# Runs of three chunks in place of four in a one-hot adjacency build

## The chip, the cores and the metric

The kernel runs on one core of one Trainium2 chip. The metric is the device time of one execution in microseconds (us), the median over several runs. Five engines work at once, each with its own instruction stream, and meet through semaphores: TensorE (PE; its weight loads are shown as PEld), VectorE (DVE), ScalarE (ACT), GpSimd (POOL) and SyncE (SP).

## The reference

The kernel computes two layers of a graph network over 3125 nodes with 256 features: a graph convolution, an attention and a feed-forward part in each. What matters here is the graph: 100,000 edges (src, dst), sorted by dst. Both graph convolutions need sums over the edges that end in a node.

```python
dst = jnp.minimum((3125 * jax.random.uniform(jax.random.fold_in(_gk, 3), (100000,)) ** 2.0).astype(jnp.int32), 49999)
_o = jnp.argsort(dst, stable=True)
src = src[_o]
dst = dst[_o]
...
def _gcn_conv(h, src, dst, norm, W, b, n):
    hw = h @ W
    msg = norm[:, None] * hw[src]
    return jax.ops.segment_sum(msg, dst, num_segments=n) + b
```

The square makes the targets uneven: low nodes have many edges, high nodes few.

## The kernel before, in words

The kernel first counts the edges between all pairs of nodes into a dense matrix, `adjacency`, in DRAM, and the graph convolutions later read it as an ordinary matrix. This case is about the stage that builds it.

The edges lie in 782 chunks of 128, one edge to a partition. The target nodes are split into 125 groups of 25 (25 tiles of TG = 5 groups). As the edges are sorted, a group's edges are a range of chunks that follow one another. A chunk at a border belongs to two groups. A preparation stage works out for each group its first chunk and its number of runs, where a run is RUN chunks and the last run of a group is filled up with chunks that aren't the group's (their keys match no column, so they add zeros). Each group has at least one run. It leaves (first, runs, runs before, runs up to) for each group in `ranges_row`, and the engines load these into registers (`ranges_of`, L469; the load is L472).

For a chunk two one-hot matrices are made: `hot_src` (128 edges x 125, the place of the source node, with a column of ones beside it for the degrees) and `hot_key` (128 x 625, target node and source block). TensorE multiplies the first by the second and adds into PSUM, in two pieces of 512 and 113 columns (L554). The engines share the work of the stage so:

- GpSimd copies a run's keys and sources into small buffers (L493, L496), up to AHEAD = 16 runs ahead.
- VectorE loops over all runs of all groups without knowing the groups. It makes the keys' one-hots of all chunks of a run (L519) and the sources' one-hots of all but the last (L516).
- ScalarE makes the source one-hot of a run's last chunk with two activations (square L577, relu L581). Group by group it also takes the finished sums out of PSUM (L590). It makes the sources of group g + 1 before it takes out group g.
- TensorE loops over the groups. For each it loads the range, waits for a free bank of sums, multiplies the block for the self-loops (L545), and then the chunks run by run.
- SyncE stores each group's sums to `adjacency` (L615).

`hot_src` and `hot_key` have RUN slots. The engines hold each other with `hot_ready` (a slot is filled) and `hot_used` (its chunk has been multiplied); chunk j of a run goes to slot j, so VectorE waits ahead of each slot until the chunk that was there one run before has been used:

```python
for j in range(RUN):
    dve.wait_ge(hot_used, n * RUN + (j + 1))
```

Behind the stage the degrees are summed from the stored matrix (L524 to L532). All stages are separated by barriers.

Of the kernel before, what the change touches and what calls it, by code (L numbers as in the profile page):

```python
# [25 lines left out]
HID = 512  # L26
E = 100000
CHUNKS = 782
RUN = 4
AHEAD = 16  # L30
CHUNKS_PAD = CHUNKS + RUN
GW = T * 25
# [43 lines left out]
def graph_kernel(nc, a, out):  # L76
    with ExitStack() as top:
# [132 lines left out]
        with ExitStack() as phase:  # L210
# [12 lines left out]
            with ExitStack() as prep, nc.Block() as block:  # L223
                def q(name, shape, dt=F32):
                    return prep.enter_context(nc.sbuf_tensor(name, shape, dt))
# [132 lines left out]
                def _(dve):  # L358
# [35 lines left out]
                    step(nc.vector.tensor_tensor(last[:], last[:], rng[:, 0:1], ALU.subtract))  # L394
                    step(nc.vector.tensor_scalar(last[:], last[:], 1.0 / RUN, (RUN - 1) / (2.0 * RUN), ALU.mult, ALU.add))
                    step(nc.vector.tensor_scalar(last[:], last[:], ROUND, ROUND, ALU.add, ALU.subtract))
# [36 lines left out]
            with ExitStack() as build, nc.Block() as block:  # L433
                def q(name, shape, dt=F32):
                    return build.enter_context(nc.sbuf_tensor(name, shape, dt))

                hot_src = q("hot_src", [128, RUN, P + 1], BF16)
                hot_key = q("hot_key", [128, RUN, GW], BF16)
                run_keys = q("run_keys", [128, AHEAD, RUN])
                run_srcs = q("run_srcs", [128, AHEAD, RUN])  # L440
                counts = q("counts", [128, TG, GW])
# [3224 lines left out]
```

How the kernel before makes its waits and increments, by code:

```python
            def __call__(self, ins, by_itself=False):  # L134
                self.n += 1
                ins.then_inc(self.sem, 1)
                if by_itself:
                    alone(self.eng, self.sem, self.base + self.n)
                else:
                    self.eng.wait_ge(self.sem, self.base + self.n)
# [7 lines left out]
            def settle(self):  # L148
                self.eng.wait_ge(self.sem, self.base + self.n)
# [14 lines left out]
        def alone(eng, signal, value):  # L164
            eng.wait_ge(signal, value)
            eng.sem_inc(waits_met, 1)
# [1 line left out]
        def load_all(eng, loads, landed):  # L170
            for dst, src in loads:
                eng.dma_start(dst, src).then_inc(landed, 16)
            eng.wait_ge(landed, 16 * len(loads))
# [18 lines left out]
            @block.gpsimd  # L192
            def _(pool):
                nc.gpsimd.memset(ident[:], 0.0).then_inc(const_made, 1)
                nc.gpsimd.memset(ones[:], 1.0).then_inc(const_made, 1)
                pool.wait_ge(const_made, 2)
                nc.gpsimd.affine_select(out=ident[:], in_=ident[:], compare_op=ALU.not_equal, fill=1.0, base=0,
                                        pattern=[[-1, 128]], channel_multiplier=1).then_inc(const_made, 1)
                pool.wait_ge(const_made, 3)
# [78 lines left out]
                @block.sync  # L278
# [1 line left out]
                    for dst, src in ((src_i, "src"), (dst_i, "dst")):  # L280
                        sp.dma_start(dst[:], a[src]).then_inc(landed, 16)
                    sp.wait_ge(cleared, 2)
                    for dst, src in ((edst_i, "edst"), (esrc_i, "esrc")):
```

## Time and profile before

| what | value |
|---|---|
| time of the kernel before, median of 3 runs | 4308.22 us (4301.39 to 4308.76) |
| span of the profiled execution | 4665.5 us |
| adjacency stage in it | 59.1 to 631.3 us, 572.2 us |
| VectorE busy in the stage | 483.1 us |
| TensorE busy in the stage | 476.0 us |
| ScalarE busy in the stage | 317.4 us |

The profiled execution is one execution with the recorder on, and no other time of its own is known than its span; it is 8.3% above the median of the timed runs. A row of the profile gives an engine, the line of the kernel, the operation with the tiles written and read, how often it ran, its busy time and the mean of one, and how long the engine stood idle just ahead of it and what ended that. Matmuls are pipelined and their ends are modelled; the starts of the weight loads (PEld) are the better marks of when TensorE went on.

### The profile page before, as it was taken

What the parts mean: (1) busy time and instruction counts of PE and PEld (TensorE: products, weight loads), DVE (VectorE), ACT (ScalarE), POOL (GpSimd) and SP (SyncE); (2) the same over time, 40 slices, a digit from 0 to 9 for tenths busy, and PEclk for the clock granted to TensorE, in tenths of its full rate; (3) what the DMA queues carried; (4) which work ended last, traced back from release to release, by engine and by line L of the source; (5) the groups of instructions that cost most, each with busy time, mean ns of one, the idle gap of its engine ahead of it and who ended that gap; (6) DMA issues with size and microseconds to landing.
All of it is one profiled execution on the core that took longest, in us unless ns stands there. A gap on an engine that the chain in (4) does not pass through costs nothing. (4 is left out here: it accounts for less than half of the span.)

```text
span 4665.5 us, 90783 instructions
## 1 busy us (share of the span) xinstructions
PE 3696.0 (79%) x23366; PEld 2634.7 (56%) x23367; DVE 2192.7 (47%) x5709; ACT 1348.5 (29%) x2983; POOL 739.5 (16%) x1224
## 2 busy tenths in 40 slices
PE   4888864899699989973464629859989899789998
PEld 2444433566388579651354416539879544457776
DVE  7888878888700221151263420270130677723333
ACT  2555532677700110320010203240000135233333
POOL 3222100000000000017423470200000466100000
PEclk9999975887799899986787859879999999989999
DMA  2111220323244024102010121224425100010000
GB/s 105 47 74 74 93 86 0 91 90 90 76 160 157 32 108 184 60 16 53 11 53 4 40 25 39 98 77 170 165 105 196 49 1 1 5 29 7 13 13 27
DMA packets 125733, 317.98 MB, mean 68 GB/s; under 512 B 43522, under 2 KB 76785, under 8 KB 111116
## 3 DMA queue, kind: packets, MB, share of 16 engines
q1 hardware_dynamic: 110404, 300.31, 18.5%
q0 software_dynamic: 11808, 9.68, 1.5%
q10 hardware_dynamic: 3404, 6.53, 0.4%
q8 instruction: 62, 1.02, 0.1%
q14 instruction: 55, 0.45, 0.0%
HBM read 244.21 MB, written 72.41 MB: 68 GB/s over the span
## 5 line engine op out<-in xcount | busy, mean ns | idle before, releaser
L554 PE MATMUL ps<-hot_key,hot_src 128*126 128x512 bf16 (+1 forms) x2208 | 416.9, 314 | 38.6 <-DVE hot_key L519 21.1
L519 DVE TENSOR_SCALAR hot_key<-col_iota,run_keys 128x625 bf16<-128x625 int16 x1104 | 393.7, 378 | 0.0
L2441 PE MATMUL ps<-xnT,ew 128*128 (+2 forms) x640 | 207.5, 479 | 206.7 <-issue 150.9
L1335 PE MATMUL ps<-gnn_u_thirds,near 125*128 125x256 bf16 x3000 | 334.7, 274 | 23.1 <-issue 23.1
L554 PEld LDWEIGHTS ps<-hot_key,hot_src 128*126 128x126 bf16 x2208 | 212.7, 136 | 234.2 <-DVE hot_key L519 171.7
L1335 PEld LDWEIGHTS ps<-gnn_u_thirds,near 125*128 125x128 bf16 x3000 | 329.7, 141 | 26.3 <-issue 24.7
L2441 PEld LDWEIGHTS ps<-xnT,ew 128*128 128x128 f32 x640 | 129.7, 210 | 279.2 <-issue 183.5
L2322 POOL DMA_INDIRECT rows_room<-node_table,src_idx x256 | 260.1, 1016 | 142.4 <-issue 142.4
L516 DVE TENSOR_SCALAR hot_src<-col_iota,run_srcs 128x125 bf16<-128x125 int16 x828 | 211.6, 256 | 97.4 <-PE ps L554 52.8
L863 PE MATMUL ps<-row_hot,slot_hot 128*128 128x512 f16 x1088 | 217.6, 351 | 3.1 <-DVE row_hot L1076 2.6
L2477 PE MATMUL ps<-table_thirds,rows_room 125*128 125x144 bf16 x1728 | 129.2, 232 | 113.9 <-issue 78.0
L2456 PE MATMUL ps<-ew,ehT 128*125 128x256 f32 x800 | 210.7, 409 | 0.0
L3620 DVE SCALAR_TENSOR_TENSOR xres<-ps,shares,xres 125x256 f32 x200 | 96.8, 484 | 239.5 <-PE ps L3585 218.6
L3574 PE MATMUL ps<-xnT,f 128*128 x640 | 185.5, 438 | 12.2 <-ACTq L3593 4.6
L1076 DVE TENSOR_SCALAR row_hot<-row_iota,row_of 128x670 f16<-128x670 int16 x544 | 189.4, 391 | 0.0
L2477 PEld LDWEIGHTS ps<-table_thirds,rows_room 125*128 125x128 bf16 x1728 | 114.2, 100 | 128.8 <-issue 128.4
L1335 PE MATMUL ps<-agg_u_thirds,near 125*128 125x257 bf16 x1500 | 175.4, 277 | 10.2 <-issue 9.7
L3574 PE MATMUL ps<-f_h1T,f 128*128 128x313 f32 (+1 forms) x640 | 180.1, 434 | 0.0
L3585 PE MATMUL ps<-fo,f_h2T 128*125 128x256 f32 x800 | 179.2, 379 | 0.0
L1335 PEld LDWEIGHTS ps<-agg_u_thirds,near 125*128 125x128 bf16 x1500 | 169.6, 141 | 16.6 <-issue 15.4
L1335 PE MATMUL ps<-gcn_u_thirds,near 125*128 125x256 bf16 x1500 | 166.6, 274 | 12.7 <-DVEq L1554 12.7
L3601 ACT ACTIVATE f_h1T<-ps,norm_shift,norm_scale 128x313 f32<-128x313 f32 (+1 forms) x160 | 98.0, 612 | 261.7 <-PE ps L3574 261.7
(570 smaller groups left out, 6651.9 us busy)
## 6 DMA issues: line engine op xcount, KB each, us to landing
near<-adjacency SPq DMA_DIRECT2D x80, 1562.5 KB, 6.6
adjacency<-counts SPq DMA_DIRECT2D x125, 312.5 KB, 2.2
own_in<-own_rows SPq DMA_DIRECT2D x34, 512.0 KB, 4.0
expert_rows<-rows_y SPq DMA_DIRECT2D x75, 125.0 KB
rows_room<-expert_rows SPq DMA_DIRECT2D x25, 375.0 KB
pair_in<-high_rows SPq DMA_DIRECT2D x34, 256.0 KB
pair_in<-low_rows SPq DMA_DIRECT2D x34, 256.0 KB
agg0a_adj<-adjacency SPq DMA_DIRECT2D x5, 1562.5 KB, 9.4
```

What stands on the lines that cost most here:

```text
L516: nc.vector.tensor_scalar(hot_src[:, j, 0:P], col_iota[:, 0:P], run_srcs[:, ds(at, 1), j:j + 1].rearrange("p a j -> p (a j)"), None, ALU.i ...
L519: nc.vector.tensor_scalar(hot_key[:, j, :], col_iota[:], run_keys[:, ds(at, 1), j:j + 1].rearrange("p a j -> p (a j)"), None, ALU.is_equal ...
L554: last = nc.tensor.matmul(sums[:, b:e], hot_src[:, j, :], hot_key[:, j, b:e], start=False, stop=True, skip_group_check=True)
L863: last = nc.tensor.matmul(ps[:, bank, 0:e - b], slot_hot[:, c % RING, :], row_hot[:, c % RING, b:e], start=False, stop=True, skip_group_ch ...
L1076: nc.vector.tensor_scalar(row_hot[:, c % RING, :], row_iota[:], row_of[i][:, c:c + 1], None, ALU.is_equal).then_inc(routes_made, 1)
L1335: last = nc.tensor.matmul(ps[:, j, 0:width], lead_tiles[BUF[j]][:, k, :], parts.thirds[:, k, i, :], start=(k == 0 and i == 0), stop=(k == ...
L2322: pool.indirect_dma_start(out=fetched[q][:, j, :], out_offset=None, in_=node_table, in_offset=bass.IndirectOffsetOnAxis(ap=src_idx[:, q, j ...
L2441: last = nc.tensor.matmul(ps[:, piece % 2, 0:n], w1[i][:, c, m * 128:(m + 1) * 128], xnT[:, c, ds(g * NG + first, n)], start=(c == 0), sto ...
L2456: last = nc.tensor.matmul(o, hT[:, c, j * P:(j + 1) * P], w2[i][:, c, :], start=False, stop=(c == 3))
L2477: last = nc.tensor.matmul(pick_bank(i, k, many)[:, slot * MIDS * HROW:(slot + 1) * MIDS * HROW], src_hot[i][0:P, tier, edges_of], table_th ...
L3574: last = nc.tensor.matmul(ps[:, piece % 2, 0:n], (w1, w2)[stage][i][:, c, m * 128:(m + 1) * 128], moving, start=(c == 0), stop=(c == 1))
L3585: last = nc.tensor.matmul(o, h2T[:, c, j * P:(j + 1) * P], wo[i][:, c, :], start=(c == 0), stop=(c == 1))
```

## The change

The constant RUN goes from 4 to 3:

```diff
-RUN = 4
+RUN = 3
 AHEAD = 16
 CHUNKS_PAD = CHUNKS + RUN
```

Everything that is written in terms of RUN follows: `hot_src` and `hot_key` have three slots; a run holds three chunks, for which VectorE makes three key one-hots and two source one-hots and ScalarE one source; the number of runs of a group is its chunks divided by three, rounded up; the small buffers of GpSimd hold three values for each run; and the edge arrays have 785 columns in place of 786.

## Rows read from the trace of the kernel before

**Rows 1.** Busy time by stretch: length, engines, granted clock, DMA share, GB/s.

```profile
59.10:631.30 572.20, 476.04 (x2456) 244.67 (x2456) 483.07 (x1932) 317.41 (x798) 121.16 (x550) 1.00 0.19 72
```

**Rows 2.** Groups of instructions in the stage (59 to 632 us).

```profile
L519 DVE TENSOR_SCALAR hot_key<-col_iota,run_keys 128x625 bf16<-128x625 int16 x1104 | 393.7, 378 | 0.0
...
L516 DVE TENSOR_SCALAR hot_src<-col_iota,run_srcs 128x125 bf16<-128x125 int16 x828 | 211.6, 256 | 97.4 <-PE ps L554 52.8 <-POOL run_keys L493 34.4 <-POOL run_srcs L496 9.7
L581 ACT ACTIVATE hot_src<-src_apart_sq,ones 128x125 bf16<-128x125 bf16 x275 | 110.5, 402 | 145.1 <-PE ps L554 127.9 <-ACT src_apart_sq L577 5.7
...
L590 ACT ACTIVATE counts<-ps 126x625 f32<-126x625 f32 x125 | 86.5, 692 | 54.9 <-PE ps L554 52.3 <-issue 2.7
```

**Rows 3.** Waits in the stage: who waited for whom, us, times, longest.

```profile
POOL run_keys L493 <- DVE hot_key L519: 415.0, 270, 2.6
```

**Rows 4.** Timeline of VectorE over one group of two runs: start, length.

```profile
407.85 0.26 DVE L516 TENSOR_SCALAR hot_src<-col_iota,run_srcs 128x125 bf16<-128x125 int16 x1 [1.10 <-PE ps L554]
408.02 0.38 DVE L519 TENSOR_SCALAR hot_key<-col_iota,run_keys 128x625 bf16<-128x625 int16 x1
408.31 0.25 DVE L516 TENSOR_SCALAR hot_src<-col_iota,run_srcs 128x125 bf16<-128x125 int16 x1
...
408.93 0.67 DVE L519 TENSOR_SCALAR hot_key<-col_iota,run_keys 128x625 bf16<-128x625 int16 x2
409.60 0.26 DVE L516 TENSOR_SCALAR hot_src<-col_iota,run_srcs 128x125 bf16<-128x125 int16 x1
...
412.06 0.26 DVE L516 TENSOR_SCALAR hot_src<-col_iota,run_srcs 128x125 bf16<-128x125 int16 x1 [0.71 <-POOL run_keys L493]
```

**Rows 5.** Timeline of TensorE's weight loads over the same group.

```profile
409.73 0.19 PEld L554 LDWEIGHTS ps<-hot_key,hot_src 128*126 128x126 bf16 x2 [0.17 <-issue]
410.73 0.26 PEld L545 LDWEIGHTS ps<-loop_blocks,own_ident 125*126 125x126 bf16 x2 [0.81 <-issue]
411.26 1.01 PEld L554 LDWEIGHTS ps<-hot_key,hot_src 128*126 128x126 bf16 x8 [0.27 <-DVE hot_key L519]
```

**Rows 6.** VectorE's sequencer (DVEq), 407.7 to 409.5 us: ns min/median/max, first and last start.

```profile
L516 DVEq FUSED_REGOPS  x4: 57/57/57, 407.7 to 409.5; - x4
...
L519 DVEq FUSED_REGOPS  x1: 57/57/57, 408.7 to 408.7; - x1
...
L508 DVEq COMPARE_BRANCH  x1: 56/56/56, 409.0 to 409.0; - x1
```

**Rows 7.** Busy time from 250 to 500 us, of L519 alone and of L590 alone.

```profile
250.00:500.00 250.00, 166.24 (x468) 1.00 0.20 76
...
250.00:500.00 250.00, 46.52 (x119) 1.00 0.20 76
```

**Rows 8.** Timeline of TensorE's weight loads, groups of one run near the end.

```profile
625.33 1.02 PEld L554 LDWEIGHTS ps<-hot_key,hot_src 128*126 128x126 bf16 x8 [0.27 <-DVE hot_key L519]
...
627.28 1.01 PEld L554 LDWEIGHTS ps<-hot_key,hot_src 128*126 128x126 bf16 x8 [0.30 <-DVE hot_key L519]
...
629.50 1.01 PEld L554 LDWEIGHTS ps<-hot_key,hot_src 128*126 128x126 bf16 x8 [0.27 <-issue]
```

**Rows 9.** Timeline of TensorE's weight loads, from one run to the next inside a group.

```profile
244.95 0.19 PEld L554 LDWEIGHTS ps<-hot_key,hot_src 128*126 128x126 bf16 x2 [0.17 <-issue]
245.66 0.46 PEld L554 LDWEIGHTS ps<-hot_key,hot_src 128*126 128x126 bf16 x4 [0.52 <-DVE hot_key L519]
```

**Rows 10.** Timeline of ScalarE over the group of rows 4.

```profile
405.50 0.40 ACT L577 ACTIVATE src_apart_sq<-col_iota,src_low 128x125 bf16<-128x125 int16 x1
406.01 0.40 ACT L581 ACTIVATE hot_src<-src_apart_sq,ones 128x125 bf16<-128x125 bf16 x1
406.64 0.40 ACT L577 ACTIVATE src_apart_sq<-col_iota,src_low 128x125 bf16<-128x125 int16 x1 [0.22 <-ACT hot_src L581]
408.39 0.40 ACT L581 ACTIVATE hot_src<-src_apart_sq,ones 128x125 bf16<-128x125 bf16 x1 [1.36 <-PE ps L554]
...
410.96 0.40 ACT L581 ACTIVATE hot_src<-src_apart_sq,ones 128x125 bf16<-128x125 bf16 x1
```

## The prediction

> **What bounds the kernel now.** I read the time by stages first: which stretch does the edit touch, and does its length reach the end of the kernel? The adjacency stage runs from 59.1 to 631.3 us and takes 572.2 us [rows 1], an eighth of the span of 4665.5. What stands ahead of it and behind it is fenced by barriers, so whatever the stage gains or loses arrives at the end one for one. The granted clock is 1.00 in it, TensorE's upper level (2.4 GHz), so the clock has nothing to give here [rows 1].
>
> Second, the groups of instructions in the stage. VectorE makes 1104 key one-hots and 828 source one-hots, ScalarE one source for each run (two activations), and there are 125 evictions, one for each group [rows 2]. 1104 is 4 x 276, and 828 is 3 x 276: the runs are padded to whole fours. No engine is full: VectorE is busy 483 us of 572, TensorE 476, ScalarE 317 [rows 1]. The reader should see there that no busy share names the bound, and look at the order of events.
>
> Third, the waits, then one group on the timeline. VectorE waits in one place, before a source one-hot: 52.8 us for TensorE, and 34.4 us that are put down to GpSimd (9.7 us more are once, ahead of the first run) [rows 2]. GpSimd runs up to 16 runs ahead and itself spends 415.0 us waiting for VectorE [rows 3], so I read those 34.4 us as waits for TensorE too: a slot comes free only when its chunk has been multiplied.
>
> The group from 407.85 to 412.06 us, two runs long, shows the circle. VectorE starts the second run at 407.85 and the first run of the next group at 409.60: 1.75 us for a run that nothing holds up [rows 4]. TensorE loads weights for the last chunk of the second run at 409.73, reads the next group's range, multiplies the self-loop block at 410.73 and loads the next group's first chunk at 411.26 [rows 5]. That frees the first slot, and VectorE goes on at 412.06 [rows 4]. The circle is 1.88 + 1.53 + 0.80 = 4.21 us, while VectorE's own work is 2 x 1.75 = 3.50. The missing 0.71 us is the wait; 125 of them are 89 us, and the waits listed are 52.8 + 34.4 = 87.2 [rows 2]. In a longer group each further run adds 1.75.
>
> So the stage should be (runs beyond two per group) x 1.75 + groups x 4.21 = (276 - 250) x 1.75 + 125 x 4.21 = 45.5 + 526.3 = 572 us. It is 572.2 [rows 1]. Two rows confirm this: between 250 and 500 us there are 468 chunks (117 runs) and 119 rows of L590, two to a group, so 59.5 groups, 4.20 us each [rows 7]. One-run groups count minus one run in this formula and should take 2.46; near the end they take 1.96 and 2.21 [rows 8], which is made up by groups at tile boundaries that take some 0.4 us more.
>
> **The change, part by part.**
>
> *How many runs.* The ranges follow from the reference's dst (seed 0), sorted and cut into chunks of 128 edges. By chunks touched: 25 groups have 4, 59 have 5 or 6, 20 have 7 or 8, 5 have 9, 8 have 10 to 12, 3 have 14 or 15, and five have 18, 20, 23, 30 and 72, 904 in all. In fours that is 276 runs, as the trace has it. In threes it is 345 runs, 1035 chunks: 69 padding chunks go, 69 runs come. No group has one run any more: 84 have two.
>
> *A run on VectorE.* One pair (source and key) goes. A pair takes 0.46 us (407.85 to 408.31) [rows 4], so at best 1.75 - 0.46 = 1.29, or 1.22 if the instructions alone counted: keys follow one another by 0.29 us and a key follows its source by 0.17, so 2 x 0.46 + 0.29 = 1.21. But VectorE's sequencer has register work as well. Its address step for the run's first source stands at 407.7, the one for the last key, three chunks on, at 408.7: 0.33 us for a chunk. Then come loop count, branch (409.0), the next run's registers and its wait, until the next run's first step at 409.5: some 0.75 [rows 6]. 3 x 0.33 + 0.75 = 1.74 is the whole run, so I read the sequencer as what sets its pace, and a chunk taken out takes only 0.33 from it: 1.42 us. I take that, since the rows leave the sequencer no pause; bounds 1.22 (the instructions alone) and 1.46 (below).
> VectorE's unhindered work is then 345 x 1.42 = 490 us against 276 x 1.75 = 483. It gains nothing, though it makes 207 instructions fewer (1035 + 690 against 1104 + 828).
>
> *The crossing from group to group.* With three slots, VectorE can be ahead of TensorE by three chunks. Of the circle, the first term ends one pair earlier (1.88 - 0.46 = 1.42); TensorE's 1.53 and the 0.80 until the slot is free are the same instructions. C = 1.42 + 1.53 + 0.80 = 3.75 us, of which VectorE works 2.84: the wait per crossing grows from 0.71 to 0.91.
>
> *Inside long groups.* TensorE's own loop needs some 0.70 us from a run's last weight load to the next run's first (244.95 to 245.66) [rows 9]. With slots one run deep, two runs then take 1.42 + 0.70 + 0.80 = 2.92 us, or 1.46 each, against 1.42. For about 70 runs that is +3 us.
>
> *Sum.* (345 - 250) x 1.42 + 125 x 3.75 + 3 = 134.9 + 468.8 + 3 = 607 us, against 572: **+35 us** in the profiled execution. By kinds of group: 25 of four chunks go from about 2.2 to 3.75 (+39), 59 of five or six from 4.21 to 3.75 (-27), 20 of seven or eight from 4.21 to 5.17 (+19), the rest near +3.
>
> *Nothing for the rest.* ScalarE makes 69 sources more, 55 us of activations at 0.40 [rows 2]. In a two-run group it needs 2.57 us from the source ahead of an eviction to the one behind it (408.39 to 410.96) and 1.14 for the other (0.62 + 0.52) [rows 10]: 3.71 against a circle of 3.75. It is hidden, by 0.04 us; without that cover every two-run group is longer by the excess. GpSimd's two operations per run (69 pairs more) lie under its 415 us of waiting [rows 3]. The stores are one per group as before, and their share of the DMA engines is 0.19 [rows 1]. The preparation works on 785 columns in place of 786, and the degrees behind the stage are untouched. The later stages see the same program.
>
> *A rule beside the rows.* VectorE sits idle 97.4 us ahead of its source one-hots [rows 2] in a stage in which TensorE also stands idle until VectorE's keys are there [rows 9]. The Trainium skill (Perfetto Trace Analysis, Optimizing Scalar/DVE Operations) says that where VectorE isn't saturated but causes bubbles on other engines, breaking up the work may let it finish sooner. By that rule smaller runs should help, and the time would be the second rival's 4273 us. The circle speaks against it, by which it is 4340: here the depth of the buffer shrinks with the run.
>
> *Onto the timed runs.* The profiled span is 4665.5 us and the median of the timed runs 4308.22, 0.923 of it. I scale: 35 x 0.923 = +32, so 4340 us.
>
> **The rivals.**
>
> 1. *Forecast: crossings and register work cost more than padding gives back*, 4340 us, chance 0.70. Its own range: low end with a run at 1.22 us, 95 x 1.22 + 468.8 = 585, +13 or 4320; high end with 0.2 us more in each of the 84 two-run groups (ScalarE's 0.04 us of cover overrun), 607 + 17, +52 or 4356.
>
> 2. *The wait at a crossing stays as it is and VectorE's work decides*: faster. If the 0.71 us per crossing didn't grow and a run took 1.29, the stage would be 345 x 1.29 + 125 x 0.71 = 534 us, 38 less: 4273. The place is TensorE's 1.53 us (range load, self-loop, loop registers). For it: that stretch is register work, and the profiled execution is 8% longer than the timed ones, so it may be shorter untimed. Against it: the formula above hits 572 with it. At 1.42 per run it decides from 3.50 us per circle down, ((572 - 135) / 125), which means a crossing shorter by 0.25 us of its 2.33 while the old kernel's doesn't shorten. Chance 0.10.
>
> 3. *ScalarE becomes the bound.* For it: 0.04 us of cover. If evictions and sources queue up by 0.3 us in each of the 84 groups, +25 on top of +35: 60 x 0.923 = +55, 4363. Against it: at 317 of 572 us it is the least loaded of the three. Chance 0.12.
>
> 4. *Nothing measurable*: the 69 chunks fewer cancel the 69 runs more, 4308. It takes a run near 1.22 and a circle near 3.65. Chance 0.08.
>
> **How the numbers follow.** About 0.2% (8.6 us) is what a measurement of this kernel tells from no change. Slower by more than that: 0.70 + 0.12 = 0.82. Same: 0.08. Faster: 0.10. The range leaves out the faster rival, most of the fourth and the far end of the third: 4312 to 4364.
>
> **What would show it.** Right: the stage lasts 600 to 615 us; 1035 key and 690 source one-hots; VectorE's undisturbed runs 1.42 us apart; two-run groups 3.75 apart; VectorE's idle time ahead of L516 up from 97.4 to about 124 us (125 x 0.91 + 9.7); later stages unchanged. Wrong: runs 1.22 to 1.29 apart (register work isn't the pace), circles under 3.50 (faster), idle time of TensorE that ends on ScalarE's L581 (third rival), or a difference outside the stage, such as another granted clock behind it.

## The result and the profile after

The changed kernel takes 4347.35 us (median of 4 runs, 4341.3 to 4351.77) against 4308.49 (median of 4: 4301.39 to 4308.76, and one of 6012.78 that the ratio leaves out). The ratio is 1.0102, 95% interval 1.009 to 1.0114: **slower by 1.0%**, 44 us by this ratio and 39 by the two medians. Forecast were 4340 us and 4312 to 4364.

The stages of the changed kernel, by stretch (length, then busy us of PE, PEld, DVE, ACT and POOL, granted clock, DMA share, GB/s):

```profile
0.00:58.60 58.60, 4.71 (x17) 2.99 (x18) 27.71 (x50) 5.74 (x10) 16.89 (x27) 1.00 0.47 171
58.60:678.00 619.40, 474.14 (x2318) 233.57 (x2318) 448.21 (x1725) 374.20 (x938) 132.07 (x688) 0.99 0.17 67
678.00:691.40 13.40, 0.40 (x1) 0.28 (x1) 4.21 (x6) 1.50 (x2) 0.38 (x1) 0.63 0.19 70
691.40:4349.20 3657.80, 3168.62 (x20842) 2376.82 (x20892) 1681.75 (x3722) 1023.29 (x2172) 616.39 (x646) 0.90 0.24 73
```

The same cuts for the kernel before:

```profile
58.90:632.00 573.10, 476.04 (x2456) 244.67 (x2456) 483.07 (x1932) 318.11 (x799) 121.16 (x550) 1.00 0.19 72
632.00:645.60 13.60, 0.40 (x1) 0.28 (x1) 4.14 (x5) 1.61 (x3) 0.38 (x1) 0.56 0.19 70
645.60:4665.50 4019.90, 3214.85 (x20892) 2386.75 (x20892) 1677.71 (x3722) 1023.04 (x2172) 601.09 (x646) 0.87 0.20 66
```

The adjacency stage went from 573.1 to 619.4 us, +46.3, while VectorE's busy time in it fell from 483 to 448 us. So the loss is waiting, not work. Ahead of the stage and in the degrees behind it nothing moved (58.6 against 58.9, 13.4 against 13.6). The last stretch differs by 362 us. I don't put that down to the change, as its program is the same. In the experiments below this stretch is 3654 to 3663 us on one chip and some 370 us longer on two others, whatever the kernel, and the kernel before takes 4307 us on the first and 4678 to 4679 on those. (Chip and time of measurement changed together, so the runs don't tell which of the two matters.) Which chip gave the profile of the kernel before isn't on record; by the length of this stretch it is one of the slower kind. Nearly all of the 362 us lie where GpSimd gathers rows by indirect DMA (L2322): the same work takes from 2097 to 3065 us before and from 2149 to 2749 us after. Times are therefore compared with runs of the kernel before on the same chip, and stages with stages.

The groups of VectorE in the stage (compare [rows 2]):

```profile
L519 DVE TENSOR_SCALAR hot_key<-col_iota,run_keys 128x625 bf16<-128x625 int16 x1035 | 363.8, 380 | 0.0
L516 DVE TENSOR_SCALAR hot_src<-col_iota,run_srcs 128x125 bf16<-128x125 int16 x690 | 177.2, 257 | 179.4 <-PE ps L554 133.0 <-POOL run_srcs L496 17.2 <-issue 10.1
```

69 keys and 138 sources fewer, as counted. The idle time in front of the sources rose from 97.4 to 179.4 us. One group of two runs on VectorE's timeline (compare [rows 4]):

```profile
510.13 0.26 DVE L516 TENSOR_SCALAR hot_src<-col_iota,run_srcs 128x125 bf16<-128x125 int16 x1 [1.04 <-PE ps L554]
510.30 0.38 DVE L519 TENSOR_SCALAR hot_key<-col_iota,run_keys 128x625 bf16<-128x625 int16 x1
510.60 0.25 DVE L516 TENSOR_SCALAR hot_src<-col_iota,run_srcs 128x125 bf16<-128x125 int16 x1
510.76 0.67 DVE L519 TENSOR_SCALAR hot_key<-col_iota,run_keys 128x625 bf16<-128x625 int16 x2
511.55 0.26 DVE L516 TENSOR_SCALAR hot_src<-col_iota,run_srcs 128x125 bf16<-128x125 int16 x1
...
513.90 0.26 DVE L516 TENSOR_SCALAR hot_src<-col_iota,run_srcs 128x125 bf16<-128x125 int16 x1 [1.05 <-PE ps L554]
```

and TensorE's weight loads beside it (compare [rows 5]):

```profile
511.56 0.19 PEld L554 LDWEIGHTS ps<-hot_key,hot_src 128*126 128x126 bf16 x2 [0.18 <-issue]
512.52 0.29 PEld L545 LDWEIGHTS ps<-loop_blocks,own_ident 125*126 125x126 bf16 x2 [0.78 <-issue]
513.10 0.74 PEld L554 LDWEIGHTS ps<-hot_key,hot_src 128*126 128x126 bf16 x6 [0.28 <-DVE hot_key L519]
```

Read the circle: 510.13 to the last chunk's load at 511.56 (1.43), to the next group's first load at 513.10 (1.54), to VectorE's restart at 513.90 (0.80): 3.77 us. A run that isn't held up takes 510.13 to 511.55, 1.42 us. The last key is done at 510.76 + 0.67 = 511.43, so VectorE's instructions leave 0.12 us unused at the end of each run.

What fills TensorE's 1.54 us is in the records of its sequencer (PEldq), 511.5 to 513.2 us, here by line with the number, the length in ns and the first and last start:

```profile
L548 PEldq COMPARE_BRANCH  x1: 76/76/76, 511.7 to 511.7; - x1
L472 PEldq TENSOR_LOAD <-ranges_row x1: 332/332/332, 511.9 to 511.9; - x1
L545 PEldq FUSED_REGOPS  x2: 46/49/52, 512.4 to 512.6; - x2
L548 PEldq MOVE  x2: 35/36/37, 512.7 to 512.8; - x2
L550 PEldq FUSED_REGOPS  x1: 50/50/50, 513.0 to 513.0; - x1
```

The loop's branch, the load of the next range, the addresses of the self-loop block and the new loop's counters follow one another about 0.1 us apart beside the 0.33 us of the range load. There is no pause in which TensorE would wait for ScalarE's eviction of the bank, although TensorE's matmul row of L545 names it. Nor does the crossing depend on how early the bank came free: into the second group of a tile, which needs the eviction of the group two before, it is 1.53 us, into the third and fourth, which need one five before, 1.54 and 1.53. Only into a tile's first group it is longer, 1.94 us, with the loop over the tiles in between.

### The profile page after: what moved, and what is told of

It is laid out like the page before. It is cut to its first block and busy times, and to the rows that moved or that the text cites. A ratio compares the mean times of both kernels' runs of the same rounds, so it can differ in the third digit from the quotient of the medians.

```text
span 4349.2 us, 92078 instructions
## 1 busy us (share of the span) xinstructions
PE 3647.9 (84%) x23178; PEld 2613.7 (60%) x23229; DVE 2161.9 (50%) x5502; ACT 1404.7 (32%) x3121; POOL 765.7 (18%) x1362
## 5 line engine op out<-in xcount | busy, mean ns | idle before, releaser
L554 PE MATMUL ps<-hot_key,hot_src 128*126 128x512 bf16 (+1 forms) x2070 | 414.9, 321 | 83.0 <-DVE hot_key L519 73.7
L554 PEld LDWEIGHTS ps<-hot_key,hot_src 128*126 128x126 bf16 x2070 | 201.5, 137 | 287.2 <-DVE hot_key L519 219.1
L519 DVE TENSOR_SCALAR hot_key<-col_iota,run_keys 128x625 bf16<-128x625 int16 x1035 | 363.8, 380 | 0.0
L2322 POOL DMA_INDIRECT rows_room<-node_table,src_idx x256 | 274.5, 1072 | 78.0 <-issue 78.0
L516 DVE TENSOR_SCALAR hot_src<-col_iota,run_srcs 128x125 bf16<-128x125 int16 x690 | 177.2, 257 | 179.4 <-PE ps L554 133.0
L2441 PE MATMUL ps<-xnT,ew 128*128 (+2 forms) x640 | 186.6, 449 | 44.4 <-ACT ehT L2539 28.3
L581 ACT ACTIVATE hot_src<-src_apart_sq,ones 128x125 bf16<-128x125 bf16 x345 | 139.0, 403 | 123.8 <-PE ps L554 102.5
```

Source lines behind the costliest of these rows:

```text
L516: nc.vector.tensor_scalar(hot_src[:, j, 0:P], col_iota[:, 0:P], run_srcs[:, ds(at, 1), j:j + 1].rearrange("p a j -> p (a j)"), None, ALU.i ...
L519: nc.vector.tensor_scalar(hot_key[:, j, :], col_iota[:], run_keys[:, ds(at, 1), j:j + 1].rearrange("p a j -> p (a j)"), None, ALU.is_equal ...
L554: last = nc.tensor.matmul(sums[:, b:e], hot_src[:, j, :], hot_key[:, j, b:e], start=False, stop=True, skip_group_check=True)
L581: nc.scalar.activation(hot_src[:, RUN - 1, 0:P], apart_sq[:], ACT.Relu, bias=ones[:, 0:1], scale=-1.0).then_inc(act_hot_ready, 1)
L2322: pool.indirect_dma_start(out=fetched[q][:, j, :], out_offset=None, in_=node_table, in_offset=bass.IndirectOffsetOnAxis(ap=src_idx[:, q, j ...
L2441: last = nc.tensor.matmul(ps[:, piece % 2, 0:n], w1[i][:, c, m * 128:(m + 1) * 128], xnT[:, c, ds(g * NG + first, n)], start=(c == 0), sto ...
```

## The experiments

Group times here are counted in the traces from one group's first weight load of L554 to the next one's, and are medians. One of the kernels leaves out part of the work; that is said there.

### The run's length in the other direction: 5, 6, 7 and 2 chunks

Four kernels that differ from the kernel before in one number.

```diff
-RUN = 4
+RUN = 5        # run5; 6 in run6, 7 in run7, 2 in run2
```

> RUN = 5, nothing else changed; the other direction of the same edit. Circle theory (a group costs one round trip between VectorE and TensorE that contains all but one of its runs, and slots as deep as a run): an undisturbed run is 4 x 0.46 + 0.29 = 2.13 us, a two-run group 4.21 + 0.46 = 4.67, the 65 groups of one run about 2.5 each; with 45 two-run, 10 three-run and 5 longer groups the stage takes about 525 us against 571, so about 4262 us. Rival, work with a fixed wait per group: 219 runs x 2.13 + 125 x 0.71 = 555 us, about 4292. Rival, padding decides (1095 chunks against 1104): no difference.

> RUN = 6, nothing else changed. Circle theory: 84 groups have one run; an undisturbed run is 5 x 0.46 + 0.29 = 2.60 us, so the one-run groups are bound by VectorE's and TensorE's own work at 2.6 to 2.8 us; the stage takes 500 to 515 us, about 4245 us. Rival, work with a fixed wait per group: 187 x 2.60 + 89 = 575 us, no gain. Rival, padding: 1122 chunks against 1104, slower by 1.6% of the stage.

> RUN = 7: 172 runs, 1204 chunks, 96 groups of one run. With runs of six VectorE was undisturbed in most groups (2.57 us a run), so no wait is left to win and each padded chunk is paid: 172 x 3.03 = 521 us plus some 10 of waits, stage 525 to 535 us, about 35 us slower than runs of six and 40 faster than before. Rival (fewer crossings keep paying): at or below the 495 us of runs of six.

> RUN = 2, the edit one step further: 484 runs, 968 chunks. Circle theory: a two-run group's circle would be 3.75 - 0.46 = 3.29 us; VectorE's undisturbed run 1.09, but TensorE's own loop (0.70 us from run to run) makes it (0.96 + 0.70 + 0.80) / 2 = 1.23; (484 - 250) x 1.23 + 125 x 3.29 + 15 = 714 us, +143 on before, about 4450 us (of a kernel before at 4308). Rival (fewer padding chunks pay once the run is short): 968 chunks x 0.437 + 125 x 0.71 = 512 us, faster than before.

Measured:

| chunks in a run | runs | undisturbed run, us | two-run group, us | stage, us | against before |
|---|---|---|---|---|---|
| 2 | 484 | none | 3.64 | 846.6 | one run, 4946.1 against 4677.8 |
| 3 (the change) | 345 | 1.42 | 3.76 | 619.4 | 1.0102 [1.009, 1.0114] |
| 4 (before) | 276 | 1.75 | 4.21 | 573.1 | 1 |
| 5 | 219 | 2.11 | 4.67 | 517.2 | 0.9869 [0.9853, 0.9886] |
| 6 | 187 | 2.57 | 5.14 | 496.9 | 0.9813 [0.9797, 0.983] |
| 7 | 172 | 3.03 | 6.04 | 527.4 | 0.9889 [0.9873, 0.9906] |

Runs of five, six and seven came out as the circle gives them: 517 against 525 expected, 497 against 500 to 515 (just below), 527 against 525 to 535. Work with a fixed wait per group (555 and 575 us) and padding are refuted: runs of five make fewer chunks than before but runs of six more, and both gain. Runs of six are the fastest version found, 4225.74 us (4224.51 to 4230.16) against 4307.06. There VectorE is all but full; the stage of runs of six, then its source group:

```profile
58.30:555.20 496.90, 431.26 (x2492) 249.04 (x2492) 484.00 (x2057) 246.82 (x621) 139.96 (x372) 1.00 0.22 83
```

```profile
L516 DVE TENSOR_SCALAR hot_src<-col_iota,run_srcs 128x125 bf16<-128x125 int16 x935 | 238.9, 255 | 20.4 <-PE ps L554 10.9 <-POOL run_srcs L496 9.2
```

484 of 497 us busy and 20.4 us of idle time in place of 97.4: with nothing left to wait for, a seventh chunk only adds padding, and runs of seven lose again.

The column of undisturbed runs tests the prediction's account of a run. It had two paces for VectorE: 0.33 us of register work for each chunk but one, plus 0.75, or 0.46 us of instructions for each chunk but one, plus 0.29 [rows 4, rows 6]. For three to seven chunks the first gives 1.41, 1.74, 2.07, 2.40 and 2.73 us, the second 1.21, 1.67, 2.13, 2.59 and 3.05. The larger of the two is 1.41, 1.74, 2.13, 2.59 and 3.05, and measured are 1.42, 1.75, 2.11, 2.57 and 3.03: up to four chunks the register work is the slower one, from five on the instructions are.

Runs of two missed: 846.6 us, where 714 were expected. The direction holds and the size doesn't. TensorE's weight loads inside a group:

```profile
400.56 0.28 PEld L554 LDWEIGHTS ps<-hot_key,hot_src 128*126 128x126 bf16 x2 [0.89 <-DVE hot_key L519]
401.04 0.34 PEld L554 LDWEIGHTS ps<-hot_key,hot_src 128*126 128x126 bf16 x2 [0.20 <-issue]
402.26 0.29 PEld L554 LDWEIGHTS ps<-hot_key,hot_src 128*126 128x126 bf16 x2 [0.89 <-DVE hot_key L519]
```

Runs follow one another by 1.70 us. I had put TensorE's loop there (1.23). What closes (that is, bounds the run) is a shorter circle: the first chunk of a run can only be made when the first chunk of the run before it, made just ahead, has been multiplied. In the kernel before that takes 0.60 (first source at 407.85 [rows 4] to the first chunk's weight load at 408.46) and 0.80 us until the slot is free, 1.40 in all. Here the two parts are 0.61 (399.95 to 400.56) and 1.09 us (to VectorE's restart at 401.65), so all of the 0.30 us more lie between a weight load and the slot that it gives back. The granted clock isn't the cause, though its mean in the stage is 0.72. It is 1.00 (the upper of the two levels, 2.4 GHz) up to 308 us, and only then lower:

```profile
58.10:308.00 249.90, 198.01 (x605) 93.60 (x606) 122.31 (x435) 125.44 (x313) 53.08 (x318) 1.00 0.06 24
308.00:904.70 596.70, 480.99 (x1580) 225.19 (x1580) 288.53 (x1018) 359.87 (x902) 106.43 (x648) 0.60 0.15 59
```

and in the first stretch the runs follow one another by 1.71 us as well, with the same two parts (0.61 and 1.10):

```profile
100.89 0.26 DVE L516 TENSOR_SCALAR hot_src<-col_iota,run_srcs 128x125 bf16<-128x125 int16 x1 [0.86 <-POOL run_srcs L496]
101.50 0.29 PEld L554 LDWEIGHTS ps<-hot_key,hot_src 128*126 128x126 bf16 x2 [0.89 <-DVE hot_key L519]
102.60 0.26 DVE L516 TENSOR_SCALAR hot_src<-col_iota,run_srcs 128x125 bf16<-128x125 int16 x1 [0.87 <-POOL run_srcs L496]
```

By their records (whose ends are modelled) the matmuls of 512 columns take 666 ns on average between 60 and 300 us, at a clock of 1.00, against 425 ns with runs of three. Why a chunk is slower here stays open.

### What sets the pace of a run: half the key

```diff
-nc.vector.tensor_scalar(hot_key[:, j, :], col_iota[:],
+nc.vector.tensor_scalar(hot_key[:, j, 0:313], col_iota[:, 0:313],
```

with RUN = 3 and the rest of `hot_key` set to zero once. The edges of the other 312 columns aren't counted.

> RUN = 3, and each key one-hot is made over 313 of the 625 columns only (the rest is set to zero once, so these edges aren't counted). What sets the pace of an undisturbed run on VectorE? Register theory: it stays at 1.42 us though the instructions take less; only the crossing shortens (two-run groups 3.75 to about 3.35), the stage falls from 618 to about 565 us. Instruction theory: an undisturbed run falls to 1.1 us or less, and the stage below 540 us.

Measured: 4321.39 us in one run against 4307.06; the stage is 584.9 us, 34 shorter than the change's 619.4 (565 were expected), and the two-run group takes 3.51 us (3.35 were expected). VectorE's timeline:

```profile
410.99 0.26 DVE L517 TENSOR_SCALAR hot_src<-col_iota,run_srcs 128x125 bf16<-128x125 int16 x1 [1.45 <-PE ps L555]
411.16 0.30 DVE L520 TENSOR_SCALAR hot_key<-col_iota,run_keys 128x313 bf16<-128x313 int16 x1
411.38 0.25 DVE L517 TENSOR_SCALAR hot_src<-col_iota,run_srcs 128x125 bf16<-128x125 int16 x1
411.54 0.51 DVE L520 TENSOR_SCALAR hot_key<-col_iota,run_keys 128x313 bf16<-128x313 int16 x2
412.41 0.26 DVE L517 TENSOR_SCALAR hot_src<-col_iota,run_srcs 128x125 bf16<-128x125 int16 x1 [0.37 <-PE ps L555]
...
414.50 0.26 DVE L517 TENSOR_SCALAR hot_src<-col_iota,run_srcs 128x125 bf16<-128x125 int16 x1 [1.04 <-PE ps L555]
```

The instructions end at 412.05, and the next run still starts at 412.41, 1.42 us behind the last, to the hundredth what it is with whole keys. The 0.37 us are put down to TensorE. But the steps of VectorE's sequencer stand at the same distances as with whole keys; those for the two sources and the next run's first one, here and in the changed kernel:

```profile
L517 DVEq FUSED_REGOPS  x3: 57/57/57, 410.9 to 412.3; - x3
L516 DVEq FUSED_REGOPS  x3: 57/57/57, 510.0 to 511.4; - x3
```

And inside long groups the runs are 1.42 us apart one after another, where the changed kernel alternates between 1.42 and 1.52. So the register work (address, counter, branch, wait) sets the pace of an undisturbed run of three. The row names a releaser that isn't it. Of the two-run group's circle only the first term got shorter, 1.18 us in place of 1.43; the expectation had taken 0.4 us from it.

### Who is in the circle: ScalarE, and TensorE's matmuls between groups

```diff
-                            if j < RUN - 1:
+                            if True:
...
-                                    if j == RUN - 1:
-                                        pe.wait_ge(act_hot_ready, before + i + 2)
...
-                        with act.Fori(0, runs) as i:
...
-                            nc.scalar.activation(hot_src[:, RUN - 1, 0:P], apart_sq[:], ACT.Relu,
-                                                 bias=ones[:, 0:1], scale=-1.0).then_inc(act_hot_ready, 1)
```

> RUN = 3, VectorE makes all three source one-hots and ScalarE none. Circle theory: ScalarE bounds nothing; the circle gets 0.17 us longer for the third source (two-run groups 3.75 to 3.9), an undisturbed run 1.42 to 1.5 us; the stage rises from 618 to 635 to 650 us. ScalarE theory (its 3.71 us per two-run group bound the stage with runs of three): the stage falls below 610 us.

(The removed loop is all of L572 to L582.) Measured: 4363.97 us in one run against 4307.06; stage 634.0 us, 15 longer than the change (635 to 650 were expected); undisturbed run 1.53 us, two-run group 3.82 (3.9 expected). Giving ScalarE's part to VectorE costs and frees nothing. As it also makes VectorE's run longer, it doesn't rule ScalarE out alone; the changed kernel's weight loads do:

```profile
L554 PEld LDWEIGHTS ps<-hot_key,hot_src 128*126 128x126 bf16 x2070 | 201.5, 137 | 287.2 <-DVE hot_key L519 219.1 <-issue 46.6 <-ACT hot_src L581 1.8
```

Only 1.8 us of TensorE's idle time end on ScalarE's source (1.2 before): the sign named for the third rival is absent. So ScalarE isn't the bound, though it had only 0.04 us of cover in the forecast.

```diff
-for b, e in ((0, 512), (512, GW)):
+for b, e in ((0, 512), (512, GW)) * 2:
     nc.tensor.matmul(sums[:, b:e], own_ident[0:P, k, :],
```

> RUN = 3, and TensorE multiplies each group's self-loop block twice (the second overwrites the first): 0.3 to 0.5 us more work between two groups. Circle theory: TensorE's crossing is part of every group's round trip, so all of it shows: 125 x 0.3 to 0.5 = +38 to +62 us on the stage of 618 us, and VectorE's wait at L516 grows by as much. Rival (VectorE's own work or ScalarE sets the stage): less than +10 us.

Measured: 4726.91 us in one run against 4677.8; stage 619.7 us, nothing on 619.4. The expectation of +38 to +62 us is refuted. The crossing in this kernel:

```profile
511.99 0.19 PEld L554 LDWEIGHTS ps<-hot_key,hot_src 128*126 128x126 bf16 x2 [0.18 <-issue]
512.97 0.47 PEld L545 LDWEIGHTS ps<-loop_blocks,own_ident 125*126 125x126 bf16 x4 [0.79 <-issue]
513.53 0.74 PEld L554 LDWEIGHTS ps<-hot_key,hot_src 128*126 128x126 bf16 x6
```

Four loads in place of two, and from the last chunk to the next group's first it is 1.54 us as in the changed kernel. The array's work lies beside the sequencer's. What I had called TensorE's work between groups is its register work: loading the range, the loop's counters, the addresses, as its records above show. The crossing is in the circle; the self-loop matmuls aren't.

### The depth of the buffers alone

Deeper, by two sets of slots used in turn (the side comes from the lowest bit of the run's number):

```diff
-hot_src = q("hot_src", [128, RUN, P + 1], BF16)
+hot_src = q("hot_src", [128, 2, RUN, P + 1], BF16)       # hot_key likewise
...
+side = n & 1                                             # on VectorE; before + i on TensorE and ScalarE
-hot_src[:, j, :], hot_key[:, j, b:e]
+hot_src[:, ds(side, 1), j, :], hot_key[:, ds(side, 1), j, b:e]
...
-pe.sem_inc(hot_used, RUN)                                # waits2 only
+pe.sem_inc(hot_used, 2 * RUN)
```

> RUN = 3 with two buffers of three slots, used in turn, so that every address is computed at run time; but the engines still wait as if there were one buffer. It measures what the addresses alone cost. All theories: no wait gets shorter, VectorE's register work per run gets longer, so an undisturbed run takes 1.5 to 1.8 us in place of 1.42 and the stage 630 to 700 us in place of 618.

> The same kernel as run3_two_waits1, with the waits of a depth of two runs (six chunks). Circle theory (the wait of VectorE at a group's end comes from slots as deep as a run): nearly all of VectorE's waits of about 115 us in the stage go, the stage is 60 to 110 us shorter than that of run3_two_waits1, and what is left is VectorE's run time (345 x 1.5 to 1.8 us) or ScalarE's 3.7 us per two-run group. Rival, the crossing is TensorE's own work (range load, self-loop, eviction) and depth doesn't matter: the stage stays within 10 us of run3_two_waits1.

> RUN = 4, two buffers of four slots, waits of a depth of two runs. Circle theory: the 89 us of waits of the kernel before go and the stage is VectorE's 276 runs at 1.75 to 2.1 us with the added register work, or ScalarE's 3.7 us per two-run group plus its work: 490 to 560 us against 571; the kernel 4230 to 4300 us. Rival (depth doesn't matter): 571 us plus the register work, 4310 us or more.

> RUN = 5, two buffers of five slots, waits of a depth of two runs. Circle theory: VectorE's 219 runs at 2.13 us (its instructions alone) or more if the register work now takes longer than the instructions, up to 2.4; the stage 470 to 530 us against 515 of RUN = 5 with one buffer; the kernel 4205 to 4260 us. Rival (depth doesn't matter): 515 us plus the register work, 4255 us or more.

Measured: 4898.08 and 4866.76 us in one run each against 4679.28, with stages of 789.8 us (run3_two_waits1) and 776.8 (run3_two_waits2), so the depth gave 13 us, where 60 to 110 were expected and under 10 from the rival. The other two: 749.8 us (1.0379 of before, [1.0362, 1.0396]) and 701.0 (1.0266, [1.0249, 1.0283]). All are far slower than with fixed slots, so these four don't decide on depth. They show something else. TensorE's loads in the stage of run3_two_waits1:

```profile
L556 PEld LDWEIGHTS ps<-hot_key,hot_src 128*126 x2070 | 295.7, 164 | 367.6 <-issue 339.4
```

339.4 us ahead of its weight loads ended on nothing but its own issue; in the changed kernel, with the slots fixed in the program, that is 46.6 us. The operands' addresses are now computed on TensorE's sequencer, and it has become the bound: with the deeper slots VectorE still waits 291.8 us for TensorE. The granted clock is lower in these stages (0.81 and 0.85; 0.96 and 0.98 with runs of four and five), so the 13 us between the first two aren't depth alone. It doesn't explain their length, though. The longest group, 24 runs at the start of the stage, runs at a clock of 1.00 in both kernels; run3_two_waits1, then the changed kernel:

```profile
59.30:107.30 48.00, 34.02 (x146) 19.48 (x146) 32.00 (x124) 19.29 (x48) 15.33 (x75) 1.00 0.10 36
59.30:96.40 37.10, 31.81 (x147) 15.15 (x148) 32.08 (x124) 19.31 (x48) 15.74 (x72) 1.00 0.13 46
```

It takes 47.7 us in place of 36.7.

Shallower, with the slots and the run of the kernel before:

```diff
-dve.wait_ge(hot_used, n * RUN + (j + 1))
+dve.wait_ge(hot_used, n * RUN + (j + 2))     # RUN = 4
```

> RUN = 4 with four slots, but VectorE waits ahead of each slot for one chunk more, so that it is never more than three chunks ahead of TensorE: the depth of the changed kernel with the run of the old one. Circle theory: the last key of the next group's first run has to wait until TensorE has crossed over, the circle gets one key and one wait longer (about 0.4 us), 125 x 0.4 = +45 to +55 us: stage about 620 us, as slow as runs of three. Rival (the run's length and its register work alone cost, not the depth): within 10 us of the kernel before.

Measured: 4766.36 us against 4677.8, ratio 1.0196 [1.0179, 1.0213]; the stage 663.2 us, +90, about twice what was expected (+45 to +55). Its keys and sources on VectorE:

```profile
L519 DVE TENSOR_SCALAR hot_key<-col_iota,run_keys 128x625 bf16<-128x625 int16 x1104 | 406.7, 380 | 83.2 <-PE ps L554 83.0
L516 DVE TENSOR_SCALAR hot_src<-col_iota,run_srcs 128x125 bf16<-128x125 int16 x828 | 212.0, 256 | 93.3 <-PE ps L554 55.4 <-issue 24.4 <-POOL run_srcs L496 13.3
```

and inside a long group:

```profile
76.93 0.26 DVE L516 TENSOR_SCALAR hot_src<-col_iota,run_srcs 128x125 bf16<-128x125 int16 x1 [0.24 <-POOL run_srcs L496]
...
78.92 0.26 DVE L516 TENSOR_SCALAR hot_src<-col_iota,run_srcs 128x125 bf16<-128x125 int16 x1 [0.24 <-POOL run_keys L493]
```

The part that I expected is the 83.0 us in front of keys, which had no idle time before: a run's last key waits until TensorE has crossed into the group. What I had left out is that this wait also closes inside a group, where the last key needs the run's own first chunk multiplied: an undisturbed run rises from 1.75 to 1.99 us. VectorE's idle time shows only behind that run, since its instructions are queued; the wait itself is in its sequencer, between the step of L512 for the last chunk and the address of the last key (77 to 78.9 us here, the run of [rows 6] below):

```profile
L512 DVEq ALU_OP  x3: 40/40/40, 77.1 to 77.7; - x3
L519 DVEq FUSED_REGOPS  x1: 57/57/57, 78.1 to 78.1; - x1
...
L512 DVEq ALU_OP  x3: 40/40/40, 408.0 to 408.7; - x3
L519 DVEq FUSED_REGOPS  x1: 57/57/57, 408.7 to 408.7; - x1
```

The two are 0.33 us apart in place of 0.09, and the 0.24 us between are the run's. The count of runs, chunks and instructions is that of the kernel before, so this loss is depth and nothing else. It is a loss of a shallower buffer; that a deeper one alone would gain isn't shown, as the kernels that tried it were bound by their addresses.

## Why the prediction was right

*The stage decides, nothing else moves.* Right: all of the difference is in the stage, and the timed 39 to 44 us are its +46.3.

*A run of three takes 1.42 us, not 1.22 to 1.29.* Right, and for the reason given: with half the key it is still 1.42. Inside long groups 1.46 was forecast, from TensorE's own loop; the group of ten runs takes 1.46 us for each run beyond two ((15.44 - 3.76) / 8), and with half the key, where that loop starts earlier, 1.42.

*The circle of a two-run group takes 3.75 us.* Right: 3.76 as a median, in the three terms forecast (1.43 + 1.54 + 0.80). The name for the second term was wrong in one respect: it is the sequencer's register work, not the matmuls.

*ScalarE is hidden* (against the third rival). Right: TensorE waits 1.8 us in all for its sources, and taking them away made the stage longer. The 0.04 us of cover was a misreading: the 2.57 us of [rows 10] contain waits for TensorE, such as the 0.39 us ahead of the eviction between the two sources, so they aren't ScalarE's own need.

```profile
409.18 0.69 ACT L590 ACTIVATE counts<-ps 126x625 f32<-126x625 f32 x1 [0.39 <-PE ps L554]
```

*Sum.* 607 us forecast for the stage, 619.4 measured. The term that was too small is 125 x 3.75. One group in five, at a tile boundary, takes 0.4 us more. I had seen that and let it stand against the 25 one-run groups that take less than the formula's 2.46 us (2.18 on average). The change does away with these one-run groups, so the boundaries stand alone: the 84 two-run groups are 3.85 us on average, +8 us; the 25 of three runs 5.25 in place of 5.17, +2; the longest 36.7 in place of 35.0, +2.

*Scaling by 0.923.* Wrong. The 357 us between the profiled span and the timed median are of the size by which the last stretch differs (362 us), most likely because the profile came from another chip than the timed runs. The stage isn't stretched with it: for runs of three it is 619.4 us in a span of 4349.2, and 619.7 with the doubled self-loop block in a span of 4725.2. Unscaled, the forecast would have been 4343.

*VectorE's idle time.* 124 us forecast, 179.4 found. The register work that I had put into the 1.42 shows in this column too: 0.12 us behind each of 345 runs, 41 us, and 10 us of tile boundaries.

*The rivals.* The faster one failed where it was said it would: the wait per crossing did not stay, and the circle is 3.76, not below 3.50. The rule named beside it, by which breaking up the work may help where VectorE causes bubbles (the Trainium skill, Perfetto Trace Analysis, Optimizing Scalar/DVE Operations), isn't borne out by smaller runs: the stage gets shorter from runs of two up to six. The rule speaks of breaking up instructions, and here every instruction keeps its size and only the batch shrinks, so no run here tests the rule itself.

## What to carry to other kernels

Where a buffer is as deep as one batch, the batch's size sets two things at once: the work per batch and how far the producer can be ahead when the consumer has something else to do. Time the whole round trip, from the producer's restart to its next, in the trace: if it is longer than the producer's own work, a larger batch pays in spite of padding, until the producer is full (here at six), and then it stops at once. Before deepening a buffer by computed addresses, look at how long each sequencer needs for them, and before scaling a profiled execution to a timed one, find the stretch in which they differ.

## What the runs showed of the hardware

- Register work sets the pace of short loops. On VectorE a loop of three chunks takes 1.42 us whether its keys have 625 columns (0.38 us) or 313 (0.30 us); from five chunks on (2.11 us) the instructions set it.
- Addresses computed at run time for both operands of TensorE's matmuls (and for VectorE's and ScalarE's writes) raised a stage with the same matmuls from 619 to 790 us.
- Two more matmuls and weight loads between groups, 125 times, cost 0.3 us in all, since the sequencer's 1.54 us were the longer part there.
- With runs of two a slot came free 1.09 us after its weight load in place of 0.80. It did so where the granted clock was 1.00 (up to 308 us) and where it was 0.60 on average (behind it) alike, so the granted clock doesn't account for it.
- The same later stretch of the program took some 370 us longer in the runs on two chips than in those on a third, while a stage of runs of three took 619.4 us in a span of 4349.2 and, with the self-loop block doubled, 619.7 us in one of 4725.2.
